# Second attention pass over a long context: scores of the keys' maxima as 32-row products in four row groups

## What is computed

```
q = (query @ Wq + bq).reshape(B, Nq, 16, 16)
k = (key   @ Wk + bk).reshape(B, 12544, 16, 16)      # key = value = context
v = (value @ Wv + bv).reshape(B, 12544, 16, 16)
attn = softmax(q k^T * 16 ** -0.5);  out = (attn v) @ Wo + bo
```

## Time and profile before

| | before |
|---|---|
| runs, median (lowest to highest) | 1117.6 us (1117.25 to 1120.2), 3 runs |
| the profiled execution | 1117.13 us, its span 1115.3 us |
| TensorE clock granted, mean | 0.994 |
| busy: TensorE, ScalarE, VectorE, GpSimd | 98%, 60%, 57%, 20% of the span |
| chain that ended last | 93% TensorE, 61% of the span on the helper's line L771 |

### The profile page before, as it was taken

One profiled execution on the slowest core, in us unless ns is written; L12 is line 12 of the kernel. 1 busy time (PEld: TensorE's weight loads), 2 busy tenths in 40 slices (PEclk: granted clock), 3 DMA queues, 4 the chain that ended last, 5 costly groups with the idle time before them and its releaser, 6 DMA issues.

```text
span 1115.3 us, 28496 instructions
## 1 busy us (share of the span) xinstructions
PE 1096.3 (98%) x9936; PEld 908.3 (81%) x9936; DVE 636.2 (57%) x1077; ACT 670.4 (60%) x1104; POOL 222.7 (20%) x317
## 2 busy tenths in 40 slices
PE   9998999999999999999989999999998999999998
PEld 7886788888888888888866888888887888888873
DVE  7999544444444444444464888888885444444342
ACT  6887334343343433334232888888888999999631
POOL 0000100000000000000104877777750210000220
PEclk9999999999999999999999999999999999999998
DMA  5453810110000111000264776777766996656290
GB/s 192 140 138 109 332 29 28 29 37 28 28 28 28 28 30 36 28 28 19 103 259 149 249 236 230 228 226 226 228 233 205 316 316 216 195 192 196 96 393 7
DMA packets 63641, 162.17 MB, mean 145 GB/s; under 512 B 6912, under 2 KB 8384, under 8 KB 58304
## 3 DMA queue, kind: packets, MB, share of 16 engines
q1 hardware_dynamic: 54736, 119.06, 33.4%
q0 software_dynamic: 8880, 42.76, 10.1%
HBM read 122.96 MB, written 38.80 MB: 145 GB/s over the span
## 4 chain that ended last, share of the span: by engine, by line
PE 93%; DVE 3%; DMA 2%; issue 1%; ACT 0%; POOL 0%; ACTq 0%; DVEq 0%; SPq 0%; POOLq 0%
PE ps L771 61%; PE ps L1039 8%; PE ps L973 8%; PE ps L819 2%; PE ps L753 1%; PE ps L834 1%; PE ps L832 1%; PE ps L830 1%; PE ps L831 1%; PE ps L833 1%; PE ps L1216 1%; PE ps L1389 1%; DMA wx<-xq_in 1%; PE ps L1409 1%; DMA q_le<-k_mem 1%
## 5 line engine op out<-in xcount | busy, mean ns | idle before, releaser
L1631 DVE TENSOR_TENSOR wide<-wide,probs 128x1024 f32<-128x1024 f32 x97 | 118.9, 1225 | 224.0 <-ACT probs L581 223.6
L1558 DVE TENSOR_TENSOR wide<-ps,wide 128x512 f32<-128x512 f32 (+1 forms) x194 | 184.9, 953 | 25.6 <-PE ps L771 22.1
L566 ACT CAST wide<-ps 128x512 bf16<-128x512 f32 x294 | 162.2, 586 | 15.6 <-PE ps L771 10.4
L581 ACT ACTIVATE probs<-ps 128x512 f32<-128x512 f32 x196 | 114.8, 599 | 79.8 <-PE ps L771 79.8
L771 PE MATMUL ps<-q_ha,t_ha 128*128 128x512 f32 x392 | 154.8, 395 | 0.4 <-ACT t_ha L556 0.4
L591 ACT ACTIVATE probs<-ps 128x1024 f32<-128x1024 f32 x132 | 128.0, 1026 | 17.3 <-PE ps L771 15.3
L1566 DVE TENSOR_TENSOR wide<-wide 128x512 bf16<-128x512 bf16 (+1 forms) x194 | 108.0, 556 | 11.5 <-ACT wide L566 1.1
L771 PE MATMUL ps<-q_ab,q_hk 128*128 128x512 f32 x392 | 106.8, 394 | 0.0
L576 ACT COPY weights_q<-ps 128x512 f32<-128x512 f32 x48 | 28.2, 588 | 105.6 <-PE ps L973 89.7
L771 PEld LDWEIGHTS ps<-q_ha,t_ha 128*128 128x128 f32 x392 | 74.4, 190 | 18.6 <-DVE wide L1558 0.8
L1619 DVE COPY v_sb<-wide 128x256 f32<-128x256 f32 x98 | 28.7, 295 | 102.0 <-PE ps L1039 100.9
(11 more groups left out here) (427 smaller groups left out, 2370.4 us busy)
## 6 DMA issues: line engine op xcount, KB each, us to landing
raw<-ctx_in SPq DMA_DIRECT2D x147, 256.0 KB, 2.7
k_mem<-q_hk SPq DMA_DIRECT2D x49, 512.0 KB, 3.0
v_mem<-probs SPq DMA_DIRECT2D x49, 256.0 KB, 3.4
wide<-v_mem SPq DMA_DIRECT2D x49, 256.0 KB, 3.9
q_le<-k_mem SPq DMA_DIRECT2D x17, 512.0 KB, 4.5
q_ab<-k_mem SPq DMA_DIRECT2D x16, 512.0 KB, 4.0
q_hk<-k_mem SPq DMA_DIRECT2D x16, 512.0 KB, 4.1
ring<-ex_in POOLq DMA_DIRECT2D x5, 1088.0 KB, 14.2
```

Of the source, the lines that this page charges most:

```text
L566: act.copy(half16[:, c:c + 512], ps[:, back_bank(layer, q) + u, :]).then_inc(sem(f"half{layer}"), 1)
L581: act.activation(e_keep[GT * slot + j][:, u * 512:(u + 1) * 512], ps[:, s_bank[j][u], :], ACT.Exp).then_inc(sem("exp0"), 1)
L1558: dve.tensor_tensor(r, scores, r, ALU.max).then_inc(sem(f"front{layer}"), 1)
L1631: dve.tensor_tensor(run[:, 0:1024], run[:, 0:1024], e, ALU.add).then_inc(sem("lsum"), 1)
```

## The change

- Scores of the second layer's first pass: keys and queries are ordered so that 32 rows (2 heads of 16) belong together. Per tile, eight products of 32 rows x 256 columns take the place of four of 128 x 512: four row groups, each with its own bank, two columns' halves (`b`). `q_ab` holds on each row its query for 2 heads (mask by row modulo 32), so zeros are only inside the 32 rows; the copies of zeros go, and GpSimd clears `q_ab` rows 96 to 127 (columns 512 on). The wait for the back banks stands in front of the whole tile.
- Keys' bias: ScalarE adds it as it takes the keys out of PSUM, in two instructions of 256 columns for the rounded keys and two for the rests. `t_e` isn't written in this layer; the fifth key product uses `t_b` and `wk_lb`.
- GpSimd makes four splits per group, in the order `t_b`, `t_ha`, low half of `t_b`, `t_la`.
- The rests' product stands between the five value products of tile 1 and those of tile 2.
- Query products 4 instead of 8 (two blocks of 128), their biases 2 instead of 4; VectorE masks in 2 instructions of 128 rows instead of 4 of 64.
- Second pass: the keys come in two DMAs of 32 partitions, each partition of four pieces of 2 KB. The 17 weight loads go one every five tiles.
- Once, under other work: VectorE's `key_parts` is shorter by six instructions, `wk_lb`'s lower half is cleared at the program's start.

```
 def values1(g, slot, first, rests=False):
...
                     last = mm(o, t_b[slot][:, ks], wv_lb[:, 0:D], 4, 5)
+                    if rests and j == 0:
+                        rests1(g, slot)

-                act.copy(ke[slot][:, 0:512], ps[:, 6, :]).then_inc(sem("keys1"), 1)
+                key_part(slot, 0).then_inc(sem("keys1"), 1)
-                act.copy(ke[slot][:, 512:1024], ps[:, 6, :]).then_inc(sem("k_lo"), 1)
+                key_part(slot, 512).then_inc(sem("k_lo"), 1)

+            def key_part(slot, at):
+                for b in range(2):
+                    bs = slice(b * GK, (b + 1) * GK)
+                    last = act.activation(ke[slot][:, at + b * GK:at + (b + 1) * GK], ps[:, 6, bs], ACT.Identity,
+                                          bias=wx1[:, XQ1["bk"] + b:XQ1["bk"] + b + 1])
+                return last

-                sp.dma_start(kp[slot][KEYS, :].bitcast(F32), k_mem[g].rearrange("a (r u) n -> (a r) (u n)", u=4))\
-                    .then_inc(sem(f"k_in{slot}"), 16)
+                for a in range(2):
+                    rs = slice(KEYS.start + 32 * a, KEYS.start + 32 * a + 32)
+                    sp.dma_start(kp[slot][rs, :].bitcast(F32).rearrange("r (u n) -> r u n", u=4),
+                                 k_mem[g, a].rearrange("(u r) n -> r u n", u=4)).then_inc(sem(f"k_in{slot}"), 16)

-                pool.tensor_tensor(t_e[slot][0:CB, :], r[0:CB, GK:2 * GK], one[0:CB], ALU.mult)
-                pool.wait_ge(sem("v_sb1"), 4 + 2 * n)
+                pool.wait_ge(sem("v_sb1"), 4 + 5 * n)
```

More of the change, by code:

```diff
@@ L45 @@
 RAW = 2 * GK
-UNITS = 4
 HEADS = (8, 16)
@@ L81 @@
 CONST = {"ident": 0, "before": 128, "causal": 256, "mask8": 384, "iota": 392, "rb": 408, "rw": 424,
[L82 to L85, removed]
+         "half": 456, "slot": 458}
+CONST["side"] = 458 + TOPK
+CONSTW = 458 + TOPK + 2
 LA = {"wq": 0, "wk": 512, "wv": 1024, "wo": 1536}
@@ L113, in perceiver @@
             t_b = [own_sb(f"t_b{s}", [P, GK], F32R) for s in range(SLOTS)]
[L114 removed]
+            t_e = [own_sb(f"t_e{s}", [CB + 1, GK], F32R) for s in range(SLOTS)]
         tiles_q = sb("tiles_q", [P, SLOTS * (RAW + 4 * GK)])
@@ L800, in query_bias @@
                 pe.wait_ge(sem("xq1_loaded"), 16)
[L801 to L804, removed]
+                for b in range(2):
+                    bq = wx1[:, XQ1["bq"] + b:XQ1["bq"] + b + 1].to_broadcast([P, P])
+                    pe.matmul(ps[:, 4 + b, 0:P], ident, bq, start=True, stop=False, skip_group_check=True)
             def queries1():
-                for u in range(UNITS):
+                for b in range(2):
                     for k in range(DK):
[L810 to L814, removed]
+                        c = XQ1["wq"] + k * D + b * P
+                        last = pe.matmul(ps[:, 4 + b, 0:P], wx1[:, c:c + P], xt[:, k * P:(k + 1) * P], start=False,
+                                         stop=(k == DK - 1), skip_group_check=True)
+                    last.then_inc(sem("q_psum"), 1)
             def rests1(g, slot):
@@ L833, in keys1, with values1 @@
                     pe.matmul(o, wk_hb[:, ws], t_b[slot][:], start=False, stop=False, skip_group_check=True)
-                    last = pe.matmul(o, wk_le[:, ws], t_e[slot][:], start=False, stop=(b == 1), skip_group_check=True)
+                    last = pe.matmul(o, wk_lb[:, ws], t_b[slot][:], start=False, stop=(b == 1), skip_group_check=True)
                 last.then_inc(sem("k1"), 1)
-            def values1(g, slot, first):
+            def values1(g, slot, first, rests=False):
                 if not first:
@@ L862, in cross, with scores1_0 @@
                     queries1()
-                def scores1(g, slot, first, after=False):
-                    if layer == 0:
-                        pe.wait_ge(sem("hi0"), g + 1)
-                    else:
-                        if not after and not (first and slot == 0):
-                            keys1(g + 1, 1 - slot, False)
-                        pe.wait_ge(sem("keys1"), g + 1)
-                    units, depth = UNITS1[layer], DEPTH1[layer]
+                def scores1_0(g, slot, first, after=False):
+                    pe.wait_ge(sem("hi0"), g + 1)
@@ L873, in scores1 @@
                     for j in range(GT):
                         t = g * GT + j
-                        q = tile_buffer(layer, slot, j)
+                        q = tile_buffer(0, slot, j)
                         ks = slice(j * P, (j + 1) * P)
-                        fresh = first and t < depth
-                        if layer == 0 and fresh and t > 0:
+                        if not (first and t < DEPTH1[0]):
+                            pe.wait_ge(sem("front0"), t - DEPTH1[0] + 1)
+                        elif t > 0:
@@ L907, in scores1 @@
-                        if layer == 1 and j == 0 and not after:
-                            rests1(g + 1, 1 - slot)
-                            values1(g + 1, 1 - slot, False)
+                        for u in range(2):
+                            cs = slice(u * 512, (u + 1) * 512)
+                            o = ps[:, (front_bank(0, q), back_bank(0, q))[u], :]
+                            if u == 1 and not (first and t < BACK1[0]):
+                                pe.wait_ge(sem("half0"), t - BACK1[0] + 1)
+                            mm(o, t_ha[slot][:, ks], q_ha[:, cs], 0, 2)
+                            mm(o, t_e[slot][0:CB + 1, ks], q_he[0:CB + 1, cs], 1, 2).then_inc(sem(("s1a_0", "s1b_0")[u]), 1)
@@ L911, in cross @@
+                scores1 = (scores1_0, scores1_1)[layer]
                 if layer == 1:
@@ L1797, in _ @@
             turned0(1)
-            for s in range(SLOTS):
-                link(dve.memset(t_e[s][CB:CB + 2, :].bitcast(F32), 1.0))
             hidden0(3)
```

126 lines of the change are left out of this document (44 added, 82 removed).

## The result

Device time of the changed kernel: **1111.4 us** median (1106.7 to 1113.3, five runs), against 1117.6 (1116.0 to 1120.2, five runs); ratio 0.9928 with a 95% interval of 0.9908 to 0.9947. That is 6 us, or 0.7%, faster; I had forecast 1087.3, and 1077 to 1106 as the range. The profiled execution is the slowest of the five, with a span of 1111.3 us.

What follows compares the result with a forecast made beforehand. TensorE's stream was taken to bound the first pass at 4.60 us a group; 4.0 over 47 groups gives -28.2, start -1.3, second pass -0.5, first microseconds +0.2: 1117.1 - 29.8 = 1087.3 us, range 1077 to 1106.

Steps and rivals of the forecast that it cites:

- The scores: First pass, TensorE: a tile's score products cost 0.55 us (0.44 to 0.65) instead of about 0.9.
- The rests between values: First pass, TensorE: behind five value products the rests no longer wait, shrinking from 0.34 plus 0.09 to about 0.22 us.
- The new wait hidden: First pass: each whole tile waits for both evictions of the tile before; each wait walked had its work in front.
- The prefetch: Second pass: spreading the later weights' loads saves 0.5 us, between 0 and some stalls of an exponential.
- row groups in line: Rival for first-pass scores: row groups run one after the other, 1.15 us a tile, run slower at 1134 us; chance 0.06.
- the lower clock: Rival: TensorE's idle time drops its clock to the 1.2 GHz level, +94 us, 1210 us; chance 0.03.
- less gain: Rival: new wait and GpSimd's meetings with VectorE hold the first-pass group at 4.2 to 4.5 us, 1097 to 1111; chance 0.23.
- keys' bias by ScalarE: First pass: two 128x256 evictions with bias take 0.65 us against 0.59 for one of 128x512, +0.06 twice per group.
- the walk: Step-by-step schedule of one first-pass group from a, the end of the second tile's back evictions: round of 3.9 us.
- a second issue and 2 KB pieces fit: Second pass: 2.3 us between key copy and first product leave room for a second load issue (0.5) and smaller pieces.
- second pass late: Rival: key loads over 2.3 us later than now stall each group, +1 x 49 us; chance 0.01.
- The added 0.1: First pass: 0.1 us added to the 3.9 group because four engines near each other rarely keep the schedule, giving 4.0.

Runs made afterwards that it cites:

- experiment 8: Changed kernel with the rests' product again ahead of all ten value products: 1123.6 us (ratio 1.005).
- experiment 9: Changed kernel with front-bank score products first and the wait for the back banks in the middle of the tile: 1108.8 us.
- experiment 10: Changed kernel without the keys' bias (one copy per eviction), plus a fifth split per group on GpSimd: 1100.7 us.
- experiment 6: Second-pass weight loads one every two tiles in the changed kernel: 1115.6 us; one every five in the kernel before: 1117.9 us.
- experiment 1: Changed kernel without the keys' bias, each keys' eviction one copy of 128x512: 1092.7 us (ratio 0.977).
- experiment 2: Changed kernel without the keys' bias, each keys' eviction two plain copies of 256 columns: 1093.0 us.
- experiment 5: Changed kernel without keys' bias, context load ahead of key store in SyncE's queue: 1088.9 us with four stores and 8 KB loads, 1089.3 with its own.

## Why the prediction was wrong

*What held.* TensorE was the bound before. The scores: I took 0.55 a tile from ends of 0.44 and 0.65, and it is 0.53 by the same count: 705.26 to 705.91, from the last full product before to the first one behind, less one step of 0.12. Of that 0.09 is the change of division ahead of them; then come two steps of 0.22, four products each. The rests between values: no wait, and experiment 8 shows that their place carries 13.5 us. The new wait hidden: experiment 9. GpSimd close to the round: experiment 10. The start: 1.1 of 1.3. The prefetch: 0.5 of 0.5 in the kernel before (experiment 6), where with one profile each luck can't be ruled out. Two of the rivals, row groups in line and the lower clock, did not come: the granted clock of the first pass is 0.99 after 1.00. The round of 4.30 lies where the rival "less gain" had it, but not for its reasons: moving the new wait changed nothing (experiment 9), and the meetings of GpSimd and VectorE are still there at 3.9 (experiment 1).

*The step that failed* is the term "keys' bias by ScalarE". I put two evictions of 128x256 with a bias at 0.65, by a row of two scaled copies of 64x256, and so the walk's keys' and rests' evictions at +0.06 each. They measure 0.84 to 0.88, +0.25 to +0.29 each, and they stand on ScalarE's chain, which the walk itself had named as next late (3.88 against 3.9). Twice 0.2 on 3.9 is 4.3, the measured round. The walk shows where it bites: it has the rests' eviction end at a+2.40, just ahead of the next keys at a+2.55 that need the same bank 6; in the trace (a = 705.41) it ends at a+2.89, and TensorE starts the keys at a+2.94. Experiment 1 gives the counterproof: with an eviction of 0.59 to 0.62 the first pass takes 201.4 us, that is 30.8 less than before and more than my 28.2. With the same two halves but no bias (experiment 2) it is 29.5 less. That puts it on the operand, not on the halving: 0.088 for each of the four activations, 0.35 a group. The Trainium skill would have priced it (ScalarE: Activation LUTs, What ACT_TABLE_LOAD costs): 186 ns plus 0.833 ns a column, and 93 ns more for each per-partition operand, which by estimate is 0.40 and 0.49 for 256 columns. The runs agree, with 0.401 and 0.489. So the mechanism was right and this size was not. I should have bounded that price from above: ScalarE was within 1% of the round, and no row of the trace before had a bias operand on such a shape. It had one on 128x128, though (L731, 0.369), where a plain copy of 128x128 takes 0.266 (L727): 0.1 more, four times a group.

*The second error* is smaller: "a second issue and 2 KB pieces fit" into 2.3 us. That compared one load's reserve with one load's delay; but with 2 KB pieces the same 183 GB/s take 0.68 of the engines' time where they took 0.56 (experiment 6), and under the later weights' loads the share reaches 1.02 (920 to 960 us), and loads come late there. The second pass takes 2 to 5 us more in most profiles and 9 in that of the result, and 199 again with 8 KB loads. Every kernel here with 2 KB pieces also loads them with two DMAs, so what the second DMA alone costs isn't shown. My "second pass late" rival named the place, at a chance of 0.01, with a threshold that was not needed.

Of the 26 us between the forecast and the profiled execution (1113.3 against 1087.3), 15 lie in the first pass and 10 in the second.

*The added 0.1* for four engines near each other stays undecided. With plain pairs of 0.65 to 0.70 (experiment 2) the group is 3.97, the walk's 3.9 with at most 0.05 more for each of the two evictions. With single copies of 0.60 (experiment 1) the same walk would give 3.8, and it is 3.92, with VectorE busy 98% of the time.

What stays open: why the second pass with 2 KB loads varies by 7 us between executions with the same instructions; I ran it again, but no edit aimed at it. A form with bias, 8 KB loads and no more issues in the queue wasn't tried.

## What to carry to other kernels

When a change frees the bound engine, the price that matters is that of the work it puts on the engine next in line; there, an operand that no row of the trace shows (here a bias) needs an upper bound of its own. Look first whether the work is needed at all: a keys' bias ahead of a softmax over the keys can be left out, and that was worth 18 us. Then look for the next engine again: without the bias it is VectorE, busy 179.8 of 180 us in experiment 5. And cost a DMA's new layout by pieces and by its place in the issuing queue, not by bytes.

## What the runs showed of the hardware that I had not expected

- An activation with a bias operand, 128x256 out of PSUM: 0.489 us against 0.401 for a copy.
- Behind two stores of 128 pieces of 2 KB whose target's outermost dimension is 4, the next store took 10.3 us to land; stores of 64 pieces with 32 rows outermost landed after 2.3 us, and the next store after 3.2.
- Eight products of 32 rows in four row groups: four start within 0.01 us, the next four 0.22 later; with the changes of division a tile costs 0.53 us.
- Key loads of 2 KB pieces in place of 8 KB ones kept the DMA engines busy 0.68 of the time at the same 183 GB/s (0.56 before).
- The meeting of GpSimd and VectorE costs both: VectorE's bf16 maximum of 128x1024 went from 0.70 to 0.85 on average in the changed kernel (single ones 1.14 and more), GpSimd's 64x256 subtraction from 0.74 to 0.82.
